# Cross-attention and a capacity-limited mixture of experts on one core: the Gelu table load moved behind a copy, scatter bounds kept in registers, x loaded in three parts on ScalarE's queue, and the engines' orders rewritten

## The reference, cut to what matters

```
x: (4, 256, 256)   ctx: (4, 256, 128)   T = 1024 tokens, E = 8 experts, capacity C = 160
q = ctx @ Wq.T + bq;  k = ctx @ Wk.T + bk
att = softmax(q @ k.T)                                 # per batch, 256 x 256
x = x + einsum('bln,bmn->blm', layernorm(x), att)
z = layernorm(x)                                       # (1024, 256)
logits = z @ gate.T;  probs = softmax(logits);  top1 = argmax(logits)
ranks  = running count of earlier tokens with the same expert; tokens with rank >= C are dropped
slots[e, rank] = z[token];  h = gelu(slots @ wi[e]);  eout = h @ wo[e]
x = x + probs[top1] * eout[top1, rank]                 # for the tokens that have a slot
```

## Time and profile before

| what | us |
|---|---|
| median of 3 runs | 114.22 (113.61 to 114.33) |
| the profiled execution | 112.16 |
| its span, first to last instruction | 110.4 |
| PE busy | 102.0 (92%) |
| DVE busy | 34.0 (31%) |
| ACT busy | 31.2 (28%) |
| POOL busy | 30.1 (27%) |

### The profile page before, as it was taken

The page is one execution under the profiler, slowest core; times in us unless marked ns, Lnnn a source line. Parts: engine busy times, 40 slices in busy tenths (PEclk is TensorE's granted clock), DMA queues, the critical chain, the costliest instruction groups (busy, mean ns, idle before and its releaser), DMA issues.

```text
span 110.4 us, 1872 instructions
## 1 busy us (share of the span) xinstructions
PE 102.0 (92%) x694; PEld 88.6 (80%) x694; DVE 34.0 (31%) x148; ACT 31.2 (28%) x81; POOL 30.1 (27%) x54
## 2 busy tenths in 40 slices
PE   5999999999979999999999999999999999999800
PEld 5685887777769989998998998569999999886400
DVE  0019999999910144500510400220020010012010
ACT  3239584329672302341041041002203104100000
POOL 6401588385873000000420120213003003021330
PEclk9999999999999999999999999999999999999997
DMA  2899999999963599999999999940001001001100
GB/s 69 247 361 328 351 331 424 422 413 414 427 266 108 132 260 368 344 319 422 419 420 417 427 416 424 424 170 13 0 0 41 6 0 48 0 0 46 48 3 5
DMA packets 7969, 25.75 MB, mean 233 GB/s; under 512 B 916, under 2 KB 4760, under 8 KB 5912
## 3 DMA queue, kind: packets, MB, share of 16 engines
q1 hardware_dynamic: 6664, 23.24, 56.5%
q0 software_dynamic: 864, 2.12, 5.2%
q10 hardware_dynamic: 432, 0.27, 1.0%
HBM read 21.14 MB, written 4.76 MB: 235 GB/s over the span
## 4 chain that ended last, share of the span: by engine, by line
PE 75%; issue 7%; POOL 6%; DVE 5%; ACT 3%; POOLq 0%; ACTq 0%; DVEq 0%
PE ps L742 70%; POOL slots_dram L301 4%; PE ps L746 2%; PE ps L739 2%; POOL rows L292 1%; ACT ez L377 1%; DVE rows L496 1%; ACT L414 1%; POOL out L332 1%; PE ps L785 1%; DVE nmax L473 1%; DVE stats L560 0%; DVE y L719 0%; DVE turner L490 0%; ACT shared L385 0%
## 5 line engine op out<-in xcount | busy, mean ns | idle before, releaser
L742 PE MATMUL ps<-shared,wi_sb 128*128 128x160 f32 x256 | 36.3, 299 | 0.7 <-ACT shared L418 0.7
L742 PE MATMUL ps<-wo_sb,shared 128*128 128x256 f32 (+1 forms) x256 | 36.1, 380 | 0.0
L742 PEld LDWEIGHTS ps<-shared,wi_sb 128*128 128x128 f32 x256 | 35.1, 190 | 1.0 <-issue 0.8
L742 PEld LDWEIGHTS ps<-wo_sb,shared 128*128 128x128 f32 (+1 forms) x256 | 27.8, 150 | 6.0 <-issue 0.7
L332 POOL DMA_INDIRECT out<-y,got x10 | 9.8, 976 | 62.9 <-DVE y L719 43.4
L428 ACT ACTIVATE shared<-ps 128x480 f32<-128x480 f32 (+1 forms) x24 | 12.6, 526 | 49.4 <-PE ps L742 49.4
L719 DVE SCALAR_TENSOR_TENSOR y<-ps,share,got 128x256 f32<-128x256 f32 x10 | 4.8, 483 | 51.6 <-PE ps L742 31.0
L301 POOL DMA_INDIRECT slots_dram<-rows,slot x8 | 8.2, 1023 | 4.6 <-DVE slot L546 1.8
L742 PE MATMUL ps<-attended,shared 128*128 128x272 f32 x32 | 8.4, 402 | 0.2 <-ACT attended L345 0.2
L742 PEld LDWEIGHTS ps<-attended,shared 128*128 128x128 f32 x32 | 5.7, 189 | 1.4 <-ACT attended L345 0.3
L832 PE MATMUL ps<-shared 128*128 128x160 f32 x32 | 5.6, 314 | 0.2 <-DVE shared L555 0.2
(11 more groups left out here) (78 smaller groups left out, 74.7 us busy)
## 6 DMA issues: line engine op xcount, KB each, us to landing
wi_sb<-in_wi SPq DMA_DIRECT2D x8, 1024.0 KB, 16.5
wo_sb<-in_wo SPq DMA_DIRECT2D x8, 1024.0 KB, 18.6
slots_dram<-fill SPq DMA_DIRECT2D x1, 1300.0 KB, 13.1
shared<-in_x SPq DMA_DIRECT2D x2, 512.0 KB, 6.7
shared<-in_xT SPq DMA_DIRECT2D x2, 512.0 KB, 7.7
out<-rows SPq DMA_DIRECT2D x4, 256.0 KB, 5.6
got<-slots_dram SPq DMA_DIRECT2D x1, 780.0 KB, 5.6
got<-slots_dram SPq DMA_DIRECT2D x4, 130.0 KB, 2.4
```

The source lines that it names most:

```text
L742: return nc.tensor.matmul(dst, lhsT, rhs, start=(k == 0), stop=last)
```

## The change

- The load of the Gelu table stands behind ACT's copy of the dispatched tokens instead of ahead of it.
- The bounds of the indirect DMAs lie in two registers that are set once at the start.
- x is loaded in three parts, tiles 0-1, 2-3 and 4-7, by ScalarE's queue, behind `small` and ahead of the load of the Exp table; SP's list loses its two x transfers.
- The lists of DVE, ACT, POOL and PE are rearranged.

```
-            context(0); context(1); inputs(0); context(2); turned_inputs(0); inputs(1); turned_inputs(1)
+            context(0); context(1); context(2); turned_inputs(0); turned_inputs(1)
```

(the same lines of SP's list, put side by side), and from the diff:

```
+X_PARTS = [(0, 2), (2, 4), (4, 8)]
+X_PART_OF = [0, 0, 1, 1, 2, 2, 2, 2]
...
+            last_slot = nc.gpsimd.alloc_register("last_slot")
+            nc.gpsimd.reg_mov(last_slot, E * CAP - 1)
...
-                    bounds_check=E * CAP - 1, oob_is_err=False).then_inc(scattered, 16)
+                    bounds_check=last_slot, oob_is_err=False).then_inc(scattered, 16)
...
             act.dma_start(small[:, W_FIRST:W_ROW], small_v[:, W_FIRST:W_ROW]).then_inc(small_here[1], 16)
+            for i, (a, z) in enumerate(X_PARTS):
+                act.dma_start(x_sb[:, a:z, :].rearrange("p (g t) h -> p g t h", t=2),
+                              x_in_v[a // 2:z // 2].rearrange("g p t h -> p g t h")).then_inc(x_here[i], 16)
             nc.scalar.preload_act_table(ACT.Exp)
...
-            nc.scalar.preload_act_table(ACT.Gelu)
 
 
             act.wait_ge(disp_done, 2)
             nc.scalar.activation(dispT[:, 1, 0, :], p_disp[1], ACT.Copy, scale=-1.0).then_inc(disp_sb, 1)
+            nc.scalar.preload_act_table(ACT.Gelu)
```

More of the change, by code:

```diff
@@ L144, in xattn_moe @@
         ctx_here = [sem(f"ctx_here{i}") for i in range(NC_)]
-        x_here = [sem(f"x_here{i}") for i in range(2)]
+        x_here = [sem(f"x_here{i}") for i in range(len(X_PARTS))]
         xT_here = [sem(f"xT_here{i}") for i in range(2)]
@@ L314, in _ @@
             shifted_input(6)
+            shifted_input(7)
             second_rstd(0)
-            shifted_input(7)
             scatter(0)
+            second_rstd(1)
             scatter(1)
-            second_rstd(1)
-            second_rstd(2)
             scatter(2)
             scatter(3)
+            second_rstd(2)
             second_rstd(3)
@@ L400, in _ @@
             at(2)
+            token(0)
             expz(0)
-            token(0)
+            token(1)
             at(3)
             expz(1)
-            token(1)
             token(2)
             token(3)
+            token(4)
             expz(2)
-            token(4)
             token(5)
+            expz(3)
             token(6)
-            expz(3)
             token(7)
-            nc.scalar.preload_act_table(ACT.Gelu)
             act.wait_ge(disp_done, 2)
             nc.scalar.activation(dispT[:, 1, 0, :], p_disp[1], ACT.Copy, scale=-1.0).then_inc(disp_sb, 1)
+            nc.scalar.preload_act_table(ACT.Gelu)
             for e in range(E):
@@ L576, in _ @@
             bn1(2)
+            bn1(3)
+            st1(0)
+            mx(0)
+            mx(1)
             gate()
-            bn1(3)
             recip(0)
+            veps1(0)
             turn_by(0)
-            st1(0)
-            mx(1)
-            veps1(0)
             bn1(4)
@@ L586, in _ @@
             bn1(6)
+            shift(0)
             bn1(7)
+            st1(1)
+            mx(2)
             recip(1)
-            shift(0)
-            mx(2)
+            veps1(1)
             turn_by(1)
-            st1(1)
-            veps1(1)
-            x1(0)
             mx(3)
             recip(2)
-            bn2(0)
             shift(1)
             turn_by(2)
+            x1(0)
+            bn2(0)
+            scaled(0)
             x1(1)
-            scaled(0)
             summed(0)
@@ L606, in _ @@
             less(0)
+            value(0)
             veps2(0)
-            value(0)
+            first(0)
             recip(3)
-            x1(2)
-            first(0)
-            bn2(2)
             chosen(0)
             turn_by(3)
+            x1(2)
+            ranks(0)
+            bn2(2)
+            place(0)
             scaled(1)
-            ranks(0)
+            x1(3)
             summed(1)
-            place(0)
+            bn2(3)
             largest(1)
-            x1(3)
+            st2(1)
+            pick(0)
             less(1)
-            bn2(3)
+            veps2(1)
             value(1)
-            st2(1)
             x1(4)
             first(1)
-            veps2(1)
+            pick(1)
             chosen(1)
-            x1(5)
             bn2(4)
             scaled(2)
-            bn2(5)
-            summed(2)
-            st2(2)
-            largest(2)
-            veps2(2)
-            ranks(1)
-            less(2)
-            pick(0)
-            pick(1)
-            place(1)
-            value(2)
+            x1(5)
+            ranks(1)
+            summed(2)
+            place(1)
+            largest(2)
+            bn2(5)
             pick(2)
             x1(6)
+            st2(2)
+            bn2(6)
+            scaled(3)
+            x1(7)
+            summed(3)
+            less(2)
+            veps2(2)
+            bn2(7)
+            value(2)
+            st2(3)
             first(2)
-            bn2(6)
-            x1(7)
-            scaled(3)
+            largest(3)
             chosen(2)
-            summed(3)
-            bn2(7)
-            largest(3)
-            st2(3)
             veps2(3)
@@ L841, in _ @@
             q(1)
+            k(1)
+            en(0)
             gate_mean()
-            en(0)
-            k(1)
-            q(2)
-            k(2)
-            en(1)
+            en(1)
+            k(2)
+            q(2)
             at(0)
@@ L868, in _ @@
             forerunners(2)
+            disp(2)
             rk(2)
-            disp(2)
             disp(3)
```

28 lines of the change are left out of this document (12 added, 16 removed).

## The result

The changed kernel takes 113.31 us (median of 7, 112.55 to 115.46); the kernel before takes 112.14 us (7 runs, the first three of them those that the prediction had): a ratio of 1.009, 95% interval 1.0058 to 1.0122. It is slower by 0.9%; forecast was a gain of 0.2 us. Several kernels here, these two among them, have some executions over 1.5% longer than their fastest; medians count them and ratios leave them out, so that 114.22, the median of the first three runs of the kernel before (113.61 to 114.33), is no level to compare 113.31 with. Profiled against profiled: 113.38 (span 111.6) against 112.16 (span 110.4), 1.2 us longer.

A forecast was written before the change was run, and what follows sets the result against it. PE, busy through the experts' 69 us, was taken as bound by its start and the slot transposes. s of -0.57 plus 0.42 gave -0.15, rounded to 0.2 off the 114.22 median: 114.0 us, range 112.7 to 115.3.

The forecast's parts named there:

- x on ScalarE's queue, statistics first: DVE's early part: statistics fill idle time; part 1 lands near 8.0, mx(0) starts at 9.15, place(1) shifts by -0.57 us.
- s: Shift of place(1)'s end on DVE against the kernel before, in us; forecast -0.57.
- What releases scatter(2): On POOL: scatter(2) waits for the slots from place(1) instead of expz(1), 0.66 us gained if place(1) stays put.
- x at 7.0: First rival, at DVE's start: x part 1 arrives early, mx(0) stays at 7.95; 113.2 or 112.9 us; chance 0.25.
- rival 3: At DVE's start: x part 1 lands behind xT, at 9.47, deciding from about 9.4 on; 115.4 us; chance 0.13.
- The bounds in registers: Scatters and output scatters lose a MOVE: 0.03 to 0.05 us at each of three waits on the path, 0.1 together.
- rival 2: At the indirect DMAs: the MOVE costs more than 29 ns, 0.5 us off each awaited one; 112.8 us; chance 0.12.
- The table load: Ahead of mm1(0): ACT's copy no longer waits for the load, 0.68 us off the first gate, none off the scatters.
- The powers: POOL's late list: second_rstd(2) behind scatter(3) makes token(7) 1.27 us and scatter(4) 1.43 us later after scatter(3).
- first gate: Start of mm1(0) on PE, after dispatch and its copy; forecast to shift by s - 0.07 us.
- s + 0.42: Forecast shift of the kernel's end: second gate's s + 0.52, less 0.1 for the MOVEs; -0.15 us in all.
- second gate: PE's transposes of the slots, waiting on the scatters; forecast to shift by s + 0.52 us, the later gate that counts.

The follow-up runs named there:

- e11: Changed kernel with x still on ScalarE's queue, but in two halves with 4 KB rows instead of three parts; 112.74 us, 1.0067 of before.
- e4: Changed kernel with x back on SP's queue in two halves, in the places of before; 111.32 us, 0.9921 of before.
- e2: Kernel before with only the bounds of the indirect DMAs put in registers; 111.28 us, 0.9927 of before.
- e5: Kernel before with the bounds in registers and the Gelu table load moved behind ACT's copy; 111.30 us, 0.9927 of before.
- e12: Changed kernel with the Gelu table load put back ahead of ACT's dispatch copy; 113.32 us, 1.0079 of before.
- e7: Kernel before with bounds in registers and the changed order of powers (POOL) and of late expz and tokens (ACT); 111.85 us, 0.9988 of before.
- e14: e4 with powers, expz and tokens back in the order of the kernel before; 113.25 us, 1.0118 of before.
- e6: e2 with the scatters' two waits exchanged, so the zeroed-rows wait sits on the DMA itself; 111.15 us, 0.9913 of before.
- e9: e4 with both halves of x ahead of xT and the scatters' two waits exchanged; 112.11 us, 0.998 of before.
- e17: e4 with the scatters' two waits exchanged as in e6; 111.54 us, 0.9961 of before.
- e18: e17 with ScalarE's read of the overflow rows ahead of its second Gelu of expert 0; 111.76 us, 0.9957 of before.
- e13: e10 with ScalarE's read of the overflow rows ahead of its second Gelu of expert 0; 112.00 us, 0.9996 of before.
- e10: e5 with the two waits exchanged for scatter(2) alone; 115.01 us, 1.0122 of before.

## Why the prediction was wrong

- **x on ScalarE's queue, statistics first** is the step that failed: part 1 of x was to be there at 8.0, and s, the shift of place(1), at -0.57; s was +0.96. Of these 1.5 us, 0.86 are mx(0) (forecast 9.15, measured 10.01), because part 1 landed at 8.91 and not at 8.0; the rest is the stretch behind it, 15.82 in place of 15.15. The removed work was oversized: DVE is busy for 14.76 where 14.35 were forecast, and it waits 0.39 for part 2 where I took 0.15. I had counted 768 KB up to part 1's landing, x and context alone. But SP's queue moved 0.78 MB between 4.0 and 8.5 us, of which context 2 is at most 0.26; the rest was xT, which I had put behind part 1 and which took its turns (388 packets to 332) while part 1 was under way. The Trainium skill ("DMA: Bandwidth & Descriptors", section "Issuing engines are not separate DMA queues") says that a second issuing engine saves only its issuing time. This much the trace bears out: it brought x no sooner. But it did change which transfer gets the bytes, as the rows of e11 show. The move as a whole cost 1.7% (e4).
- **What releases scatter(2)** was wrong too. The sum had it wait for place(1), so that scatter(3) would end at -0.66 + s, which is +0.30 with the measured s; it ended at -0.05, because scatter(2) came right behind scatter(1). The late x reached the scatters over place(0), 1.55 late, and POOL's list behind it; place(1) was done 0.26 before scatter(1) ended and held nothing up.
- The arrival had its rivals at both ends (x at 7.0, or behind xT from 9.4 on). The landing of 8.91 lay between my value and rival 3's threshold; no rival had it. That 113.31 lies between the range's ends, 112.7 and 115.3, is owed to the width that the rivals gave it and not to this step.
- **The bounds in registers**: 0.03 to 0.05 for each wait was wrong, **rival 2** (0.5 each) right where the wait itself moved to the DMA. That is one of the three places counted. At the tail it gave 0.5, at scatter(2), whose wait stayed on an instruction ahead, 0.06; in all 0.8 us (e2). I had taken the MOVE's 29 ns for the price of the step; the time lies between a met wait on an instruction ahead and the start of the DMA, which no row of the MOVE shows.
- **The table load**: direction right (worth nothing at the end), size of its gate wrong: 0.41 at most, since ACT's copy needs the later half of dispatch. e5 and e12 agree.
- **The powers**: the order of events was right to within 0.1 us: scatter(2) no longer waits for expz(1), POOL's powers start when scatter(3) ends, scatter(4) 2.30 after that (forecast 2.37), token(7) 3.30 (3.29). With DVE's old order they cost 0.6% (e7). What I missed is that they had to move with DVE's order (e14).
- **The gates**: first gate s - 0.07 was forecast, 0.97 measured with s = 0.96. The second did bind (0.87 in place of 0.60 for the transposes). A third, the long read of the slots, had no term and took 0.5 more; in this profile the read took 6.8 us from issue to landing against 5.6, and in e12's, where it took 5.2, PE did not wait there. The end came 1.2 after before's, where s + 0.42 would have been 1.38: given s, the sum was close by luck. The second gate came 0.24 less late than s + 0.52, the missing gate added 0.5, and the registers gave 0.5 at the tail where 0.1 was counted for all of them.
- The level of 114.0 came within 0.7 of 113.31 for the wrong reason: it was hung on a median of 114.22 that the later runs put at 112.14. From 112.14 the same sum gives 111.9, 1.4 below.

## What to carry to other kernels

Moving statistics into idle time ties the next operation to their input; check the landing of that input under the new queue order. Here two busy queues shared by packets, so that the transfer with the shorter rows got fewer bytes, and what used to stand behind x now went beside it. An order in one engine's list is not an edit of its own: undo it alone, and the engine may wait 2 us at the head of its list for something that the other list has moved. A faster producer can lose, too: when scatters end ahead of an instruction behind which a read is queued on another engine, that read can land with the long one and not ahead of it.

## What the runs showed of the hardware

- An indirect DMA on POOL that carries the awaited semaphore itself started 0.27 to 0.30 us after the event (output scatter in e2, scatter(2) in e6 and e7), scatter(4) 0.35 to 0.44 (e9, e17, e18); behind a waiting MOVE or another waiting instruction it was 0.77 to 0.84, and 0.87 to 0.95 for scatter(0). Back to back scatters started 1.27 to 1.35 apart, the first two 1.53.
- Packets of two hardware queues went in near equal number (41 and 40 between 3.5 and 4.5 us in the changed kernel, 332 and 388 between 4.0 and 8.5, 234 and 267 in e11), the bytes by the size of a row.
- A read of 130 KB that went out 0.01 behind SP's first landed 2.8 to 3.0 us later (before, e5, e13); 0.3 to 1.1 behind SP's first it took 6.4 and 5.2 (e17, e10), and PE waited 3.01 and 1.88 for it. That this is also what makes the executions of 114.1 to 114.7 of the kernel before is possible, since in its profiled execution the scatters ended only 0.2 us after the second Gelu began; no trace of such an execution was taken, and it stays open.
